# Order of loads, splits and exponentials at the start and at the seam of a fused attention and FFN kernel

## What is computed

```python
xn = (x - mean) / sqrt(var + 1e-5)
# s: "attention" within each token, over the 16 places of a head, 8 kv heads, q summed over groups of 4
q, k, v = xn @ Wq + bq, xn @ Wk + bk, xn @ Wv + bv
s = softmax(q k^T / 4) v
# g: FFN of inner width 1792
nx = xn * rsqrt(mean(xn**2) + 1e-5) * ln_w
g = silu((silu(nx @ gate.T) * (nx @ up.T)) @ down.T)
out = x + s * g
```

## Time and profile before

| | |
|---|---|
| median of 3 runs (lowest to highest) | 480.94 us (480.83 to 482.02) |
| the profiled execution, its own time | 480.94 us |
| its span, first to last instruction | 479.2 us |
| PE busy | 468.6 us (98%), 2122 matmuls |
| DVE busy | 411.2 us (86%) |
| ACT busy | 243.8 us (51%) |
| POOL busy | 121.6 us (25%) |
| mean granted TensorE clock | 0.996 |

### The profile page before, as it was taken

How to read it: one execution, slowest core, us unless ns; L and a number is a source line. 1 busy time by engine, 2 the same in 40 slices (tenths; PEclk the granted TensorE clock), 3 DMA queues, 4 the chain that set the end, 5 groups by cost and what they waited for, 6 DMA issues and landing times.

```text
span 479.2 us, 6217 instructions
## 1 busy us (share of the span) xinstructions
PE 468.6 (98%) x2122; PEld 391.2 (82%) x2122; DVE 411.2 (86%) x561; ACT 243.8 (51%) x417; POOL 121.6 (25%) x106
## 2 busy tenths in 40 slices
PE   7999999999999999999799999999999999999997
PEld 6898888888887888888687888888888888888886
DVE  6889778987898898888966898899998888888994
ACT  4785666558688888653212245335335334448102
POOL 5740213216222222133235011111111111126920
PEclk9999999999999999999999999999999999999999
DMA  8606997569689966563247558656556655514772
GB/s 270 246 1 230 355 378 263 222 190 306 212 254 307 420 271 253 178 215 122 89 128 269 218 198 316 255 197 221 219 198 220 219 198 198 197 44 133 261 266 88
DMA packets 44623, 105.70 MB, mean 221 GB/s; under 512 B 20272, under 2 KB 21808, under 8 KB 41264
## 3 DMA queue, kind: packets, MB, share of 16 engines
q1 hardware_dynamic: 44592, 105.31, 61.9%
HBM read 69.90 MB, written 35.40 MB: 220 GB/s over the span
## 4 chain that ended last, share of the span: by engine, by line
PE 85%; DMA 3%; DVE 3%; ACT 2%; SPq 2%; issue 2%; POOL 1%; ACTq 0%; POOLq 0%
PE gu_ps L553 16%; PE gu_ps L555 16%; PE gu_ps L556 16%; PE y_ps L687 7%; PE y_ps L689 7%; PE y_ps L688 7%; PE gu_ps L689 3%; PE gu_ps L688 3%; PE gu_ps L687 3%; PE gu_ps L718 2%; PE gu_ps L715 2%; PE gu_ps L714 2%; DMA raw<-down 2%; SPq L319 1%; DMA norm_kept<-norm_out 1%
## 5 line engine op out<-in xcount | busy, mean ns | idle before, releaser
L553 PE MATMUL gu_ps<-z_hi,w_ops 128*128 128x512 f32 x378 | 147.4, 390 | 0.3 <-ACT u L891 0.3
L555 PE MATMUL gu_ps<-z_lo,w_ops 128*128 128x512 f32 x378 | 147.1, 389 | 0.0
L556 PE MATMUL gu_ps<-z_hi,w_ops 128*128 128x512 f32 x378 | 147.1, 389 | 0.0
L498 POOL TENSOR_TENSOR h_lo<-h,h_hi 128x512 fp32r<-128x512 f32 x28 | 37.2, 1330 | 228.5 <-ACT h_hi L916 228.3
L553 PEld LDWEIGHTS gu_ps<-z_hi,w_ops 128*128 128x128 f32 x378 | 71.0, 188 | 16.2 <-ACT u L891 1.1
L556 PEld LDWEIGHTS gu_ps<-z_hi,w_ops 128*128 128x128 f32 x378 | 71.0, 188 | 14.7
L555 PEld LDWEIGHTS gu_ps<-z_lo,w_ops 128*128 128x128 f32 x378 | 71.0, 188 | 14.6
L687 PE MATMUL y_ps<-wd_ops,h_hi 128*128 128x512 f32 x168 | 66.4, 395 | 3.4 <-POOL h_lo L498 3.4
L689 PE MATMUL y_ps<-wd_ops,h_lo 128*128 128x512 f32 x168 | 66.2, 394 | 0.0
L688 PE MATMUL y_ps<-wd_ops,h_hi 128*128 128x512 f32 x168 | 66.2, 394 | 0.0
L916 ACT ACTIVATE h_hi<-h 128x512 fp32r<-128x512 f32 x28 | 17.7, 630 | 62.3 <-DVE h L1211 62.3
(11 more groups left out here) (139 smaller groups left out, 753.6 us busy)
## 6 DMA issues: line engine op xcount, KB each, us to landing
w_kept<-w_ops SPq DMA_DIRECT2D x13, 1792.0 KB, 6.1
w_ops<-w_kept SPq DMA_DIRECT2D x13, 1792.0 KB, 7.5
wd_ops<-wd_kept SPq DMA_DIRECT2D x35, 512.0 KB, 3.8
raw<-gate_up SPq DMA_DIRECT2D x30, 256.0 KB, 5.0
wd_kept<-wd_ops SPq DMA_DIRECT2D x14, 512.0 KB, 7.7
xz<-x SPq DMA_DIRECT2D x16, 256.0 KB, 5.2
raw<-down SPq DMA_DIRECT2D x14, 256.0 KB, 8.2
w_ops<-wd_kept SPq DMA_DIRECT2D x7, 512.0 KB, 7.5
```

The source lines that it names most:

```text
L498: pool.tensor_tensor(lo, src, hi.bitcast(F32), ALU.subtract).then_inc(h_lo_done, 1)
L553: pe.matmul(acc, w_h, z_hi[:, zi, c, :], start=start and c == 0, stop=False, skip_group_check=True)
L555: pe.matmul(acc, w_h, z_lo[:, zi, c, :], start=False, stop=False, skip_group_check=True)
L556: end = pe.matmul(acc, w_l, z_hi[:, zi, c, :], start=False, stop=c == 1, skip_group_check=True)
```

## The change

Six edits. (1) SyncE loads x's tiles 0 and 1, ln_w and gate, then tiles 2 and 3, up, and only then Wq. (2) `first_gate0` makes its high x high part tile by tile, with the transposes of tiles 2 and 3 between. (3) The low part of the first gate weights goes from VectorE to GpSimd, as a product with ln_w (between the scales of tiles 1 and 2) and a difference; GpSimd's sums of queries go ahead of the rms; `w_lo_a` counts one less. (4) ScalarE's `first_hi(1)` goes ahead of two copies of z, VectorE's `x_variance(0)` behind the last normalisation. (5) In the groups 6 to 9 the spread loads go behind the stores and down's load. (6) In the seam: `QKV_BEHIND`, `BURST_SHARES`, the places of `t_add`, and the exponentials of group NI, which go from the seam's run into the first group behind it.

```diff
+        def lo_pieces(n):
+            return n + 1
...
-        QKV_BEHIND = (0, 1, 2, 4, 6)
+        QKV_BEHIND = (1, 3, 5, 7, 9)
...
-        BURST_SHARES = (0, 0, 2, 1, 4, 5, 7, 3, 3, 2)
+        BURST_SHARES = (0, 0, 2, 6, 5, 5, 4, 3, 2)
...
-                    sp.wait_ge(w_lo_a, a_pieces(n - 2))
+                    if n == 2:
+                        sp.wait_ge(first_lo_done, 2)
+                    sp.wait_ge(w_lo_a, lo_pieces(n - 2))
...
-            load_x(0, range(0, J))
+            load_x(0, (0, 1))
             sp.dma_start(lnw_sb[:], lnw).then_inc(lnw_in, 16)
             load_gate(0)
+            load_x(0, (2, 3))
+            load_up(0)
             for a in (0, 2):
                 sp.dma_start(wq_raw[:, a:a + 2, :], wq.rearrange("(k p) n -> p k n", p=P)[:, a:a + 2, :])\
                   .then_inc(wq_in[a // 2], 16)
-            load_up(0)
...
-                if 6 <= g < 10:
-                    load_spread((g - 6) // 2, ((0, 1), (2, 3))[g % 2])
                 if g:
                     keep_w(g)
                     keep_wd(g - 1)
                     if g + 1 < NI:
                         load_down(g + 1)
+                if 6 <= g < 10:
+                    load_spread((g - 6) // 2, ((0, 1), (2, 3))[g % 2])
...
-            for j in range(J):
-                scale_tile(j)
+            def first_gate_scaled():
+                pool.wait_ge(lnw_in, 16)
+                pool.wait_ge(gate_in[0], 16)
+                pool.tensor_tensor(w_sum[:, 0:2, :].rearrange("p m (c n) -> p (m c) n", n=P), gu_raw[:, 0, 0:K, :],
+                                   lnw_sb[:].unsqueeze(2).to_broadcast([P, K, P]), ALU.mult).then_inc(first_lo_done, 1)
+            def first_gate_lo():
+                pool.wait_ge(w_hi_a, 1)
+                pool.wait_ge(first_lo_done, 1)
+                pool.tensor_tensor(w_ops[:, 0, 1, WA11:WA22, :], w_sum[:, 0:2, :],
+                                   w_ops[:, 0, 0, WA11:WA22, :].bitcast(F32), ALU.subtract).then_inc(first_lo_done, 1)
+            scale_tile(0)
+            scale_tile(1)
+            first_gate_scaled()
+            scale_tile(2)
+            scale_tile(3)
+            first_gate_lo()
+            sum_queries(0)
+            sum_queries(1)
             pool.wait_ge(var_done, J + 1)
             rms_of(0, J, 1, 0)
-            sum_queries(0)
-            sum_queries(1)
             scale_tile(J)
...
-                pe.wait_ge(z_hi_done, J)
-                for n, (wi, zi, c) in enumerate(chunks):
-                    pe.matmul(acc, w_ops[:, 0, 0, wi, c * P:(c + 1) * P], z_hi[:, zi, c, :], start=n == 0, stop=False)
-                pe.wait_ge(w_lo_a, 1)
+                for j in range(J):
+                    pe.wait_ge(z_hi_done, j + 1)
+                    t = slice(j * P, (j + 1) * P)
+                    for n, (wi, zi, c) in enumerate(chunks):
+                        pe.matmul(acc[:, t], w_ops[:, 0, 0, wi, c * P:(c + 1) * P], z_hi[:, zi, c, t],
+                                  start=j == n == 0, stop=False, skip_group_check=True)
+                    if j + 2 < J:
+                        transpose_tile(y_ps[:, j + 2, :], j + 2)
+                pe.wait_ge(first_lo_done, 2)
...
-            for j in range(J):
-                transpose_tile(y_ps[:, j, :], j)
+            transpose_tile(y_ps[:, 0, :], 0)
+            transpose_tile(y_ps[:, 1, :], 1)
...
             for j in range(J):
                 z_hi_tile(j)
+            first_hi(1)
             z_raw_tile(0)
             z_raw_tile(1)
-            first_hi(1)
...
-                if u == NI + 4:
-                    exps(exps_in(NI))
...
-                if g > NI:
-                    exps(exps_in(g))
+                exps(exps_in(g))
                 h_hi_part(item_of(1, 0, g - NI))
...
-            x_variance(0)
             normalise_tile(J - 1)
-            first_lo(0)
+            x_variance(0)
             for j in range(J):
                 z_lo_tile(j)
-            first_lo(1)
+            first_up_lo()
...
-                if n in (1, 3):
-                    t_add(1, n - 1)
-                    t_add(1, n)
+                if n in (1, 2):
+                    t_add(1, 2 * n - 2)
+                    t_add(1, 2 * n - 1)
```

More of the change, by code:

```diff
@@ L174, in build @@
         w_summed, w_lo_a, w_lo_s = sem("w_summed"), sem("w_lo_a"), sem("w_lo_s")
+        first_lo_done = sem("first_lo_done")
         bn_done, stats_done, var_done, z_done = sem("bn_done"), sem("stats_done"), sem("var_done"), sem("z_done")
@@ L353, in keep_w @@
             def keep_w(n):
-                sp.wait_ge(w_lo_a, a_pieces(n))
+                sp.wait_ge(w_lo_a, lo_pieces(n))
                 wait(sp, w_lo_s, n)
@@ L561, in need_a @@
                 if g <= NI:
-                    pe.wait_ge(w_lo_a, a_pieces(g))
+                    pe.wait_ge(w_lo_a, lo_pieces(g))
                 else:
@@ L580, in first_gate0 @@
                 pe.wait_ge(w_hi_a, 1)
-                pe.wait_ge(z_hi_done, J)
-                for n, (wi, zi, c) in enumerate(chunks):
-                    pe.matmul(acc, w_ops[:, 0, 0, wi, c * P:(c + 1) * P], z_hi[:, zi, c, :], start=n == 0, stop=False)
-                pe.wait_ge(w_lo_a, 1)
+                for j in range(J):
[7 more added lines that the diff above has]
+                pe.wait_ge(first_lo_done, 2)
                 for wi, zi, c in chunks:
-                    pe.matmul(acc, w_ops[:, 0, 1, wi, c * P:(c + 1) * P], z_hi[:, zi, c, :], start=False, stop=False)
+                    pe.matmul(acc, w_ops[:, 0, 1, wi, c * P:(c + 1) * P], z_hi[:, zi, c, :], start=False, stop=False,
+                              skip_group_check=True)
                 pe.wait_ge(z_lo_done, J)
@@ L589, in first_gate0 @@
                     end = pe.matmul(acc, w_ops[:, 0, 0, wi, c * P:(c + 1) * P], z_lo[:, zi, c, :], start=False,
-                                    stop=n == 3)
+                                    stop=n == 3, skip_group_check=True)
                 end.then_inc(m2_done, 1)
@@ L600, in first_up0 @@
                     pe.matmul(acc, w_h, z_lo[:, zi, c, :], start=False, stop=False)
-                pe.wait_ge(w_lo_a, 2)
+                pe.wait_ge(w_lo_a, 1)
                 for n, (wi, zi, c) in enumerate(chunks):
@@ L936, in y_out @@
                 if f == 0:
-                    act.wait_ge(w_lo_a, a_pieces(NI))
+                    act.wait_ge(w_lo_a, lo_pieces(NI))
                     act.wait_ge(w_summed, 4 * NI)
@@ L1163, in sums, with first_up_lo @@
                 dve.tensor_tensor(w_sum[:, 3, :], a12, w_sum[:, 1, :], ALU.subtract).then_inc(w_summed, 1)
-            def first_lo(part):
-                dve.wait_ge(w_hi_a, part + 1)
-                for m, c, k in first_places(part):
+            def first_up_lo():
+                dve.wait_ge(w_hi_a, 2)
+                for m, c, k in first_places(1):
                     t = slice(c * P, (c + 1) * P)
@@ L1303, in _ @@
             normalise_tile(J - 2)
+            normalise_tile(J - 1)
             x_variance(0)
-            normalise_tile(J - 1)
-            first_lo(0)
             for j in range(J):
                 z_lo_tile(j)
-            first_lo(1)
+            first_up_lo()
             for j in range(J, JJ):
```

## The result

| | before | after |
|---|---|---|
| median (lowest to highest), us | 481.10 (480.83 to 482.02), 4 runs | 476.74 (476.45 to 477.13), 4 runs |
| ratio after / before | | 0.9906, 95% interval 0.9889 to 0.9924 |
| profiled execution and its span | 480.94, 479.2 | 477.13, 475.3 |
| PE, DVE, ACT, POOL busy | 468.6, 411.2, 243.8, 121.6 | 467.1, 413.3, 243.7, 125.1 |
| mean granted clock of the profiled execution | 0.996 | 0.996 (1.000 in the three others) |

The kernel is faster by 4.4 us; forecast were 475.9 us and a range of 474.0 to 478.5. The page of the profile gives the busy times and the chain of work that ended last, of which TensorE now has 97% instead of 85%.

The account below looks back on a forecast made before the run. TensorE was taken to bound the kernel, with only its idle time and half clock (seam, middle, start) open to change. Seam -5.6, spread loads -0.4 and start +1.0 took 480.94 to 475.9 us, range 474.0 to 478.5.

Parts of the forecast that it names:

- Step 1: Seam between x's halves: moved exponentials and respaced qkv products end stall, half clock and short waits; -5.6 us (-4.3 to -5.8).
- Rival C: Seam: h's low part is late for another reason than the exponentials, so the stall stays; 480.5 us, chance 0.05.
- Step 2: Groups 6 to 9: later spread loads end ScalarE's wait for down's load near 144 us; -0.4 us (-0.5 to +0.3).
- Step 3: Start: later x tiles and GpSimd's longer list cost more than is won back; +1.0 us (-0.7 to +2.8).
- both of its own signs: Start: wrong if up's first matmul comes before 14.5 or after 17 us, or if the clock falls there.
- Tile 2's landing: Start: x's tile 2, now fourth in bytes, lands at 6.7 us, later by 1.37.
- rival A: Start costs nothing: tile 2's load is not held by bytes, lands by 5.8; 474.6 us, chance 0.14.
- The narrow quarters: Start: 128-column gate matmuls cost 0.11 us each, the pace of the transposes; four narrow ones 0.45.
- tile 4's chain: Start: GpSimd's scale at 17.7, tile 4 ready for transposes 19.7 to 20.4 against TensorE's 20.4; even, some delay likely.
- Rival D: Start: GpSimd's queue becomes the bound, its work stretched 1.8 times beside VectorE; slower, 483.2 us, chance 0.03.
- page's rule of section 4.1: Start: two-input work is about half as fast on GpSimd; by it 1.0 us more is lost, 476.9 us.
- Rival B: Start: TensorE falls to half clock, eight matmuls at 0.43 instead of 0.23; +1.6, 477.5 us, chance 0.12.

Follow-up runs that it names:

- exps_only: Kernel before with only the exponentials of group NI moved from the seam to the first group behind it; 475.94 us, ratio 0.9889.
- order_only: Kernel before with the new QKV_BEHIND, BURST_SHARES and t_add places, exponentials still in the seam; 482.92 us, ratio 1.0030.
- seam_spread: Kernel before with only the seam and spread-load edits, start unchanged; 474.67 us, ratio 0.9871; repeated on another chip 474.81, ratio 0.9860.
- experiment 1: The seam_spread run: seam and spread-load edits alone on the kernel before; 474.67 us, ratio 0.9871.
- loads_x_first: Changed kernel with x's four tiles loaded first again, ahead of ln_w and gate; 475.42 us, ratio 0.9891.
- warm_46: Changed kernel with 46 warm-up transposes instead of 32; 476.51 us, ratio 0.9909.
- pool_late: Changed kernel with GpSimd's product of gate and ln_w behind scale 3 instead of between scales 1 and 2; 476.57 us, ratio 0.9898.
- low_on_vector: Changed kernel with the first gate weights' low part back on VectorE and GpSimd's two added operations gone; 480.34 us, ratio 0.9986.
- experiment 3: Changed kernel with gate's low part back on VectorE: low_on_vector, 480.34 us; the same with x's four tiles loaded first, 475.57 us.
- pool_list_x_first: loads_x_first with GpSimd's product of gate and ln_w behind scale 3 and the rms behind tile 4's scale; 476.19 us, ratio 0.9892.
- Experiment 2: The loads_x_first run: changed kernel with x's four tiles loaded first again; 475.42 us, ratio 0.9891.
- seam_spread_up_early: seam_spread with ScalarE's first_hi(1) ahead of the copies of z; 474.79 us, ratio 0.9860.

## Why the prediction was right, and which terms were off

**Step 1, the seam: right in mechanism and size.** 213.07 to 259.34 is 46.27 us against the 46.4 of 13 x 2.76 + 5 x 2.10, a gain of 5.75 against 5.6. No down product waits in this stretch, the clock is 1.00, and ScalarE's run fitted at its new place with 0.74 us to spare, 0.8 being forecast. exps_only shows the cause (the exponentials waited for scores that came late), order_only that the new order alone loses 1.2 us (482.92 against 481.77). The move of the exponentials alone gives 5.8, all of the term; the new places of the q/k/v products, which the prediction counted on as a part of it, added nothing that the times show. Rival C is out: the run that moved the exponentials alone had no stall.

**Step 2, the spread: right, with one thing missed.** The ratio of 0.9979 is -1.0 us, with an interval of -0.3 to -1.7; -0.4 was forecast, and after's own marks leave 0.5 for the groups. The wait that I saw near 145 did go. I hadn't named what can be late next, two groups on, behind spread loads that now stand ahead of down's load. In after too ScalarE waits there; in seam_spread, with the same queue, no such wait is listed, so it comes and goes from run to run:

```profile
145.56 0.62 ACT L861 ACTIVATE wd_ops<-raw 128x512 fp32r<-128x512 f32 x1
...
171.20 0.63 ACT L861 ACTIVATE wd_ops<-raw 128x512 fp32r<-128x512 f32 x1 [1.11 <-DMA raw<-down]
```

**Step 3, the start: right in sign, mis-sized.** +1.0 was forecast; experiment 1 gives +2.07 (1.7 by the ratios), within the bounds of -0.7 to +2.8. The miss of 0.8 us (476.74 against 475.9) is this 1.07, less 0.27 that seam and spread gave beyond the forecast (480.94 - 474.67 = 6.27 against 6.0); part of the total's nearness is this offset. Up's first matmul came at 17.62, not at 15.5, outside what I had allowed (14.5 to 17), and the clock fell there in the profiled execution: by both of its own signs the prediction was wrong in this step. The timelines part the term into the landing of x's tile 2 and all the rest (us):

| | tile 2's statistics start | up's first matmul | group 1's first product | from the statistics to group 1 |
|---|---|---|---|---|
| before | 5.37 | 14.29 | 41.95 | 36.58 |
| seam_spread | 5.51 | 14.40 | 42.05 | 36.54 |
| loads_x_first | 5.47 | 15.77 | 42.51 | 37.04 |
| warm_46 | 6.95 | 16.93 | 43.64 | 36.69 |
| pool_late | 7.11 | 16.70 | 43.83 | 36.72 |
| after | 7.65 | 17.62 | 44.36 | 36.71 |
| low_on_vector | 7.36 | 19.54 | 47.74 | 40.38 |

With the changed loads the end of the start follows the landing one to one: 36.7 us behind it in after, in warm_46 with the clock up, and in pool_late with GpSimd's product moved. (low_on_vector's 40.4 holds the two waits and the lower clock of experiment 3.) Against before the landing is 1.6 to 2.3 later and the rest 0.1 to 0.2. The forecast had 1.37 for the landing and so -0.4 for the rest. In its sum the landing was thus 0.2 to 0.9 short and the rest 0.5. Three things in the term:
- *Tile 2's landing.* I took 6.7 us. It landed at 7.63 in after, at 6.9 in warm_46, 7.08 in pool_late and 7.34 in low_on_vector. "Loads land in order and at the pace of their bytes" was of use against rival A, but gave a poor number. Nor does one number hold for one load order: with x first tile 2 landed at 5.34 in before, 5.44 in loads_x_first and 6.29 in pool_list_x_first. Experiment 2 prices the order of loads: 0.7 to 1.3 us.
- *VectorE beside GpSimd.* I kept the durations of VectorE's list and let only GpSimd's scales be late. But the normalisation, 0.54 to 0.56 us before, took 0.92 beside the new product (9.86 to 10.78; GpSimd's operation ended at 10.49), and the next two 2.01 (to 13.23, GpSimd's difference ending at 12.94); x_var took 1.00 instead of 0.16, to 14.15, where GpSimd's sum ended at 14.13. Each of them ended 0.0 to 0.3 us after a 128x512 operation of GpSimd. So the last normalisation ended at 13.2, where I had 11.5, and z's low part began at 14.06. As the rest is only 0.1 to 0.2 us in the table, what was won back (the 1.13 us of low part, the quarters) must nearly have paid for this hold. The hold could have been read before the change: the same low part that took 1.13 us at 9.68 takes 1.98 for up's weights, beside GpSimd's sums, in the timeline of the kernel before:

```profile
13.84 1.98 DVE L1169 SCALAR_TENSOR_TENSOR w_ops<-raw,lnw_sb,w_ops 128x128 fp32r<-128x128 f32 x4 [0.64 <-ACT w_ops L807]
```

- *The narrow quarters.* Their price was right: four in a row took 0.64 us at full clock, at the pace of the transposes that I had taken.

Two smaller terms: tile 4's chain, from which I took the last 0.2 us, cost nothing, as TensorE has no wait for tile 4 in after or in loads_x_first. Its scale was forecast for 17.7 and started at 19.53. The recorded 19.7 to 20.4 for this chain adds up to 19.6 to 20.2.

**Rival D in reverse.** I had priced GpSimd being stretched by VectorE, 1.8 times. Its product took 1.03 us, the 1.05 of the earlier trace rows, its difference 1.27, and VectorE was the one held. (Later GpSimd was stretched too, beside the two-input low part of qkv on VectorE: the rms product took 0.83 us against 0.20 in before, tile 4's scale 1.26 in both.) That an operation keeps the port for its whole length and the other engine waits is what the Trainium skill says in "SBUF — State Buffer", SBUF: two separate sides, and the ends above agree with it; the page puts VectorE's part of this down to operations with two SBUF inputs or in a fast mode that uses both ports. The gate's low part has two inputs in SBUF, and page and rows agree (2.45 us against 1.13 in low_on_vector). The normalisations and x_var have a single tensor input and were held too; no run shows in which mode they ran, so whether the page's condition covers them stays open. Not every one-input operation was held: z_var, one column wide, kept 0.15 us at 9.79, inside the product's 9.46 to 10.49. On GpSimd's side operations of 128x512 and 128x256 did this (in low_on_vector x_var took 0.62 us, to 12.85, where the 128x256 sum ended at 12.83); beside the 128x1 scale at 7.76 VectorE's normalisation kept 0.54 to 0.55, and beside the 128x4 rms of before at 9.29 the last one kept 0.56.

**GpSimd for the low part.** The page's rule of section 4.1 of "GPSIMD Engine Reference" in the Trainium skill, that two-input work belongs on VectorE, would have put after at 476.9, and the median is 476.7; that is luck, as the reason is another. Putting the work back on VectorE does not win 1.0 us, it loses 3.6 with these loads (2.5 of it by the lower clock on twelve matmuls) and wins nothing with x first. The rule prices an operation; here VectorE's list was the chain and GpSimd's was not.

**Rival B** did happen in the profiled execution (four narrow quarters and the transposes at clock 0.50 for 3.4 us), in one of four runs, and costs 0.7 at most: the chain of the start was VectorE's, so half-speed matmuls filled TensorE's idle time. In the table after, with the drop, has the 36.7 us of warm_46, without it. I had 1.6 for it. Nor did the rule on idleness that I cited decide the case: one kernel with one list of work had the drop in one execution and not in three. Where the drop reached the wide matmuls behind the chain, in low_on_vector, it did cost 2.5. **Rival A** is out, by the landings.

**A faster kernel.** seam_spread, the change without its start, is the best of all: 474.67 and 474.81 us on two chips, ratios 0.9871 and 0.9860 against 0.9906 for the whole change. seam_spread_up_early, with one edit of the start, is level with it (474.79).

**What stays open.** What the remaining 0.5 to 0.75 us of loads_x_first is. Its marks place it ahead of up's first matmul: that is 1.37 us later than in seam_spread (15.77 against 14.40), of which 0.46 is left at group 1. The held normalisations (0.7 and 0.9 us) lie there. The longer list ahead of tile 4's scale does not: TensorE has no wait for tile 4 in this run. That the holds are the cause is argued, not shown; the one run meant to show it had a wait of its own, and no other was made. Nor do I know why tile 2 landed at 7.63 in one run and at 6.9 in another of the same load order.

## What to carry to other kernels

A step that waits for another engine's late result, and has the main chain's work queued behind it, belongs where it has slack: the move of one such run was worth 5.8 us of 481, and reordering everything around it made things worse without the move and added nothing measurable to it. When loads are reordered at the start, follow the tile that becomes late through every list behind it, and price each edit by itself: four edits of the start cost about 2 us inside a change that won 4.4 as a whole. When work is given to GpSimd, look at which of VectorE's operations will run beside it, not only at its own duration.

## What the runs showed of the hardware

- Some of VectorE's one-input operations are held beside GpSimd's 128x512 and 128x256 ones: a 128x512 normalisation went from 0.54 to 0.92 and 1.23 us, a 128x4 operation from 0.16 to 1.00 and 0.62; a 128x1 one kept 0.15. Low parts with two inputs in SBUF went from 1.13 to 1.98 and 2.45. Work that reads PSUM was not held: z's low part took 2.47 us for four, 0.62 each, beside the same sums, and 1.88 for three in before.
- What follows a stall differs: after 2.97 us of wait the granted clock of the next 4.5 us was 0.62, after 5.29 us it was 0.50 for 4.7 us, and with two waits of 0.90 and 0.80 us in a thinly used stretch it was 0.50 for 6.8 us.
- Of the same kernel one execution had the lower clock at the start and three had not, which moved the time by 0.7 us at most.
- One order of loads doesn't give one landing: x's tile 2 was there between 5.34 and 6.29 us with x first, between 6.9 and 7.63 with it behind ln_w and gate. In after, warm_46 and pool_late what follows moved with it one to one.
